# One layer of causal attention and routed experts: 64-row operands in 128-partition transfers, and steps moved

## The chip, the cores and the metric

The kernel runs on one core of one Trainium2 chip. The metric is the device time of one execution in microseconds (us), lower is better. A core has five engines that run their own instruction streams and meet at semaphores: TensorE (PE, matrix products), VectorE (DVE), ScalarE (ACT), GpSimd (POOL) and SyncE (SP, which here only issues transfers).

## The reference

For 8 batches of 512 tokens and 128 features the output is x plus causal attention plus a mixture of experts, both on the layer norm of x:

```python
xn = _layernorm(x, axis=-1)
x = x + attention(xn) + ffn(xn)
# attention: 16 heads of 8 features
q, k, v = split(xn @ w_in.T + b_in)
attn = softmax(q * scale @ k.T + causal_bias)
out = (attn @ v) @ w_out.T + b_out          # NaN replaced by 0
# ffn: 8 experts of width 176, the best 2 of a token count, and shared experts of width 352
scores = softmax(x @ gate_w.T); topk_w = topk_w / topk_w.sum() * 2.5
y = sum_e combine[:, e] * (silu(x @ w_gate[e]) * (x @ w_up[e])) @ w_down[e]
y = y + (silu(x @ sw_gate) * (x @ sw_up)) @ sw_down
```

## The kernel before

The kernel works batch by batch. A batch i has two stages. `attend(i)` (L686 on PE, L807 on ACT, L949 on POOL, L1287 on DVE) computes 20 units of transposed scores (`scores_t`, L570), exponentiates each (L821), masks them on POOL (L946) and multiplies them with v (`weigh_v`, L605); beside it the tokens of batch i+1 get their projections, their splits into bf16 parts and their routing weights. `experts_and_maxima(b)` (L648 on PE, L1246 on DVE, `experts` L780 on ACT and L912 on POOL) runs the hidden features of the experts of batch b in 14 tiles, k = 0 to 13, and the row maxima of batch b's scores, 20 pairs of heads (`pair`, of `scores` L518 and `maxima` L1158), between them. PE's order inside a step k of that loop is: `gate_up(k)`, the pairs of the step, at k = 14 `project_k`, `scores_t(b, 0, 0)`, `project_v_and_logits`, at k = 15 `scores_t(b, 0, 1)`, then `down(k - 2)`, and at k = 12 (`MAXIMA_AT`) `transpose_x` and `transpose_maxima`.

A tile k goes gate_up (PE) -> silu (ACT, L763) -> times the routing weight, on POOL, if the tile is routed (L902) -> `hidden`, times up (DVE, L1141) -> high part (ACT L770, the last two DVE L1149) -> low part (POOL L908, the last three DVE L1156) -> down (PE, L495 to L497). Tiles 0 to 10 are routed, 11 to 13 shared; tile 13 has 96 rows. The order of all batches is 11, 12, 13, 0, ..., 10.

Scores are products of q and k that are split into three bf16 parts each: 6 products of parts (`TERMS`) times 8 features make 48 rows for a head, and the head's parity picks partitions 0 or 64. The parts go out to DRAM (`k_parts_out`, `q_parts_out`, L341 and L346) and come back as rows of `q_op` and `k_op` (`operands_in`, L362), in two halves of four transfers, each of 48 partitions. The maxima are reduced by DVE, split into three bf16 parts (`split_maxima`, L1175, four dependent instructions of 64 columns), transposed by PE (L555), copied by ACT into `max_rows` (L791), and brought by two transfers into three further rows of q_op for each parity (`maxima_in`, L382); rows 48 to 50 of k_op hold ones. `scores_t` waits for that (L574).

SP works through one queue in program order: parts out, first half of the operands, routing weights out to DRAM and back as `cb` (L360, 18 transfers a batch), second half, output, maxima. In the first batch ACT issues the routing weights itself (`weights_out`, L772), after high_hidden(2), and waits for them to be in DRAM before its next instruction. DVE normalises the tokens of the next batch (`normalise`, L1033) at the start of `experts_and_maxima`, ahead of the first maximum; only for the second batch it does it at k = 9.

Until the seventh maximum pair the pairs use one slot of PSUM, so that each `scores` waits until DVE has read the pair before it (L538).

## Time and profile before

| | us |
|---|---|
| median of 3 runs (612.55 to 613.24) | 613.1 |
| the profiled execution | 613.62 |
| its span on the core | 611.8 |
| PE busy | 534.0 (87%) |
| DVE busy | 489.3 (80%) |
| ACT busy | 342.0 (56%) |
| POOL busy | 343.9 (56%) |
| granted TensorE clock, mean | 0.973 |

Seven batches follow each other at 69.9 us (the first maximum pair of two neighbours starts at 390.24 and 460.17), after a start of some 37 us and the first batch's experts, and the last batch's attend stage ends the run. A stretch in the rows below gives its length and the busy time of each engine with the number of instructions, then the granted clock, the busy share of the 16 DMA engines and GB/s. A row of the timeline has the start, the duration, the engine, the line, the operation with its tiles and shapes, and in brackets how long the engine was idle before it and what ended that. Matmuls are pipelined: two of 0.39 us follow each other 0.23 us apart.

### The profile page before, as it was taken

The page shows a single profiled execution, that of the slowest core. Times are in us where ns is not written, and L with a number is a line of the kernel's source. Part 1 is how long each engine was busy: PE and PEld are TensorE (multiplying, and loading weights), DVE is VectorE, ACT ScalarE, POOL GpSimd, SP SyncE. Part 2 cuts the span into 40 slices and gives each one's busy share as a digit, 9 for nine tenths or more (in the row PEclk, how much of TensorE's full clock was granted, in tenths as well). Part 3 has the DMA queues.
Part 4 walks back from the last instruction along what each step waited for, and adds up shares of the span by engine and source line. Part 5 has one row for each costly group of instructions (what it writes and reads, how often), then busy time and mean ns, then how long its engine had stood idle before and what let it go on. Part 6 is the DMA issues. An engine that isn't in the chain of part 4 may idle for free.

```text
span 611.8 us, 13262 instructions
## 1 busy us (share of the span) xinstructions
PE 534.0 (87%) x4568; PEld 299.5 (49%) x4568; DVE 489.3 (80%) x802; ACT 342.0 (56%) x462; POOL 343.9 (56%) x363
## 2 busy tenths in 40 slices
PE   2737989997899989999898989899898998999894
PEld 2415742665326662466425663366525663366422
DVE  5956978899778978799778978799778988589513
ACT  5412378453883459534793459634694358734591
POOL 3145735385365854478355864568355773568442
PEclk9768999999999999999999999999999999999897
DMA  9655014700238003730147003630048003460001
GB/s 274 190 169 116 2 56 126 218 7 0 94 104 217 7 4 130 187 95 0 52 129 233 3 3 109 184 119 0 3 155 228 29 0 108 129 183 2 4 1 34
DMA packets 43198, 56.65 MB, mean 93 GB/s; under 512 B 4545, under 2 KB 28577, under 8 KB 43169
## 3 DMA queue, kind: packets, MB, share of 16 engines
q1 hardware_dynamic: 40460, 53.02, 29.6%
q10 hardware_dynamic: 2708, 3.24, 1.6%
q8 instruction: 18, 0.29, 0.2%
q14 instruction: 12, 0.09, 0.1%
HBM read 41.05 MB, written 14.81 MB: 91 GB/s over the span
## 4 chain that ended last, share of the span: by engine, by line
PE 56%; DVE 14%; ACT 10%; issue 8%; DMA 5%; POOL 4%; SPq 1%; ACTq 1%; DVEq 0%; POOLq 0%
PE banks L617 10%; PE banks L514 7%; PE banks L479 6%; ACT probs L821 6%; DVE neg_max L1166 6%; PE banks L590 6%; PE banks L481 5%; PE banks L480 5%; PE banks L495 5%; DMA q_op<-max_rows 3%; PE banks L496 3%; PE banks L497 3%; POOL hid_lo L908 2%; DVE probs L1141 2%; POOL probs L902 2%
## 5 line engine op out<-in xcount | busy, mean ns | idle before, releaser
L1166 DVE TENSOR_REDUCE neg_max<-banks 128x2 f32<-128x1024 f32 (+3 forms) x224 | 194.9, 915 | 15.4 <-PE banks L505 14.1
L821 ACT ACTIVATE probs<-banks 128x1024 f32<-128x1024 f32 x160 | 155.5, 1031 | 23.0 <-PE banks L590 20.8
L902 POOL TENSOR_TENSOR probs<-probs,cb 128x512 f32<-128x512 f32 x88 | 112.9, 1283 | 79.2 <-ACT probs L763 71.0
L946 POOL TENSOR_SCALAR_AFFINE_SELECT probs<-probs 128x512 f32<-128x512 f32 x128 | 91.6, 739 | 112.1 <-ACT probs L821 112.1
L763 ACT ACTIVATE probs<-banks 128x512 f32<-128x512 f32 (+1 forms) x112 | 66.9, 598 | 153.0 <-PE banks L481 145.8
L908 POOL TENSOR_TENSOR hid_lo<-probs,hid_hi 128x512 fp32r<-128x512 f32 (+1 forms) x88 | 113.5, 1289 | 62.0 <-ACT hid_hi L770 62.0
L1141 DVE TENSOR_TENSOR probs<-probs,banks 128x512 f32<-128x512 f32 (+1 forms) x112 | 75.9, 679 | 28.6 <-POOL probs L902 26.2
L479 PE MATMUL banks<-x_hi,w_hi 128*128 128x512 f32 (+1 forms) x224 | 94.5, 422 | 4.1 <-DVE probs L1141 2.4
L617 PE MATMUL banks<-probs,v_op 128*32 128x512 f32 (+3 forms) x1024 | 95.5, 445 | 0.6 <-POOL probs L946 0.4
L770 ACT ACTIVATE hid_hi<-probs 128x512 fp32r<-128x512 f32 (+1 forms) x96 | 60.5, 630 | 58.6 <-DVE probs L1141 58.1
L480 PE MATMUL banks<-x_lo,w_hi 128*128 128x512 f32 (+1 forms) x224 | 89.0, 397 | 0.0
L481 PE MATMUL banks<-x_hi,w_lo 128*128 128x512 f32 (+1 forms) x224 | 88.8, 396 | 0.0
L590 PE MATMUL banks<-q_op,k_op 51*128 51x384 bf16 (+3 forms) x512 | 63.0, 303 | 21.9 <-DMA q_op<-max_rows 11.4
L514 PE MATMUL banks<-k_op,q_op 48*64 48x512 bf16 (+3 forms) x1024 | 61.8, 310 | 20.6 <-DVE neg_max L1166 16.4
L590 PEld LDWEIGHTS banks<-q_op,k_op 51*128 51x128 bf16 x512 | 17.4, 94 | 95.4 <-ACT probs L821 56.9
L495 PE MATMUL banks<-hid_hi,wd_hi 128*128 128x512 f32 (+1 forms) x112 | 55.9, 499 | 9.2 <-POOL hid_lo L908 9.0
L514 PEld LDWEIGHTS banks<-k_op,q_op 48*64 48x64 bf16 x1024 | 24.3, 106 | 59.7 <-issue 57.3
L479 PEld LDWEIGHTS banks<-x_hi,w_hi 128*128 128x128 f32 (+1 forms) x224 | 42.3, 189 | 22.5 <-issue 6.8
L481 PEld LDWEIGHTS banks<-x_hi,w_lo 128*128 128x128 f32 (+1 forms) x224 | 42.4, 189 | 10.5
L480 PEld LDWEIGHTS banks<-x_lo,w_hi 128*128 128x128 f32 (+1 forms) x224 | 42.5, 190 | 8.4 <-issue 0.2
L497 PE MATMUL banks<-hid_lo,wd_hi 128*128 128x512 f32 (+1 forms) x112 | 45.2, 403 | 0.0
L496 PE MATMUL banks<-hid_hi,wd_lo 128*128 128x512 f32 (+1 forms) x112 | 45.2, 403 | 0.0
(122 smaller groups left out, 599.9 us busy)
## 6 DMA issues: line engine op xcount, KB each, us to landing
cb<-c_dram SPq DMA_DIRECT2D x31, 256.0 KB, 4.3
q_op<-q_dram SPq DMA_DIRECT2D x32, 192.0 KB
k_op<-k_dram SPq DMA_DIRECT2D x32, 192.0 KB
cb<-c_dram SPq DMA_DIRECT2D x16, 224.0 KB, 4.9
q_dram<-q_parts SPq DMA_DIRECT2D x8, 384.0 KB, 2.5
k_dram<-k_parts SPq DMA_DIRECT2D x8, 384.0 KB, 2.6
cb<-c_dram SPq DMA_DIRECT2D x16, 192.0 KB, 4.1
cb<-c_dram SPq DMA_DIRECT2D x15, 160.0 KB, 4.4
```

The source lines that it names most:

```text
L479: pe.matmul(bank, w_hi[:, w, cols], x_hi[:, :], start=True, stop=False)
L480: pe.matmul(bank, w_hi[:, w, cols], x_lo[:, :], start=False, stop=False)
L481: pe.matmul(bank, w_lo[:, w, cols], x_hi[:, :], start=False, stop=True).then_inc(ready, 1)
L514: pe.matmul(bank[rows, a, at:at + n], q_op[own, h // 2, qt * P + HALF * c:qt * P + HALF * (c + 1)], k_op[own, h // 2, 0:n], start=first, s ...
L590: mm = pe.matmul(bank[:, at:at + S - kb * P], k_op[r:r + rows, h // 2, kb * P:(kb + 1) * P], q_op[r:r + rows, h // 2, kb * P:S], start=Tru ...
L617: mm = pe.matmul(bank[32 * j:32 * j + 32, kb * P:S], v_op[:, kb, g % 2, 4 * (g // 2) + j, :], probs_of(g, j, kb), start=(c == 0 and g % 2 ...
L821: nc.scalar.activation(probs[:, g % 2, 2 * u:2 * u + 2, :], ring[:, at:at + 2, :], ACT.Exp).then_inc(exp_done, 1)
L902: nc.gpsimd.tensor_tensor(sg[k % 3][:, :], sg[k % 3][:, :], cb[:, tiles_of(b)[k], :], ALU.mult).then_inc(weighted, 1)
L908: nc.gpsimd.tensor_tensor(hid_lo[0:n, k % 3, :], hid[k % 3][0:n, :], hid_hi[0:n, k % 3, :].bitcast(F32), ALU.subtract).then_inc(hid_lo_don ...
L946: return nc.gpsimd.affine_select(out=view, in_=view, compare_op=ALU.is_ge, fill=0.0, base=0, pattern=[[0, 4], [1, P]], channel_multiplier=-1)
L1141: nc.vector.tensor_tensor(hid[k % 3][0:n, :], sg[k % 3][0:n, :], ring[0:n, up_bank(k), :], ALU.mult).then_inc(hid_done, 1)
L1166: return nc.vector.tensor_reduce(out, in_, AX.X, ALU.max, negate=True)
```

## The change

- Heads get 64 rows, 8 slots for each of the 8 features, laid out feature by feature (row = 8 d + slot): slots 0 to 5 the products, slot 6 the maxima, slot 7 nothing (q 0, k 1). q_dram and k_dram have 8 slots; slots 6 and 7 are written once at the start by two transfers from memory set by POOL. `operands_in` issues two transfers of 128 partitions instead of four of 48. `maxima_in` issues one transfer, into 16 partitions, from a `max_rows` of 128 rows of which 5 of 8 are zero.
- `split_maxima` has seven dependent `tensor_reduce` (copies over an axis of one, subtraction as the sum of two, one of them negated) instead of two copies and two subtractions.
- Batches after the first take their tiles as 11, 12, 0, ..., 10, 13.
- At k = 12 PE transposes the maxima ahead of down(10) and transpose_x; ACT copies max_rows ahead of high_hidden and take_xT. `project_v_and_logits` stands ahead of `scores_t(b, 0, 0)`; take_k ahead of the first exponential, exp_router after the second.
- For batches 2 to 6 `normalise` stands in attend, after the routing weights, instead of at the start of the experts.
- First batch: the split of one half of the routed weights (`low_routed(1)`), the high part of the down weights on ACT, the routing weights and their way out each stand elsewhere: router_weights at k = 1, transpose_comb at k = 2 behind down(0), weights_out after high_hidden(1), `low_down` on POOL waits for routed_lo.

```diff
-TILES_LATER = TILES_FIRST
+TILES_LATER = list(range(ROUTED, NT - 1)) + list(range(ROUTED)) + [NT - 1]
...
-                for s in range(2):
-                    rows = slice(HALF * s, HALF * s + SROWS)
-                    sp.dma_start(q_op[rows, own, :], q_dram[:, s, :, own, :]).then_inc(ops_loaded[n], 16)
-                    sp.dma_start(k_op[rows, own, :], k_dram[:, s, :, own, :]).then_inc(ops_loaded[n], 16)
+                for op, dram in ((q_op, q_dram), (k_op, k_dram)):
+                    sp.dma_start(op[:, own, :].rearrange("p i n -> p (i n)"),
+                                 dram[:, :, :, own, :].rearrange("t s d i n -> (s d) t (i n)")
+                                 ).then_inc(ops_loaded[n], 16)
...
-                for s in range(2):
-                    row, own = HALF * s + SROWS, MROWS * PAIRS * s
-                    sp.dma_start(q_op[row:row + MROWS, :, :], max_rows[own:own + MROWS * PAIRS, :]
-                                 ).then_inc(m_loaded, 16)
+                sp.dma_start(q_op[TERMS:P:SLOTS, :, :], max_rows[:, :]).then_inc(m_loaded, 16)
...
+            sp.wait_ge(slots_set, 3)
+            sp.dma_start(q_dram[TERMS:SLOTS].rearrange("t s d i n -> (s d i) t n"), q_op[:, 0:SLOTS - TERMS, :]
+                         ).then_inc(slots_written, 16)
+            sp.dma_start(k_dram[TERMS:SLOTS].rearrange("t s d i n -> (s d i) t n"), k_op[:, 0:SLOTS - TERMS, :]
+                         ).then_inc(slots_written, 16)
...
                     if k == NT:
                         if front:
                             project_k(b + 1)
+                            project_v_and_logits(b + 1, vl)
                         scores_t(b, 0, 0)
-                        if front:
-                            project_v_and_logits(b + 1, vl)
                     if k == NT + 1:
                         scores_t(b, 0, 1)
+                    if k == MAXIMA_AT:
+                        transpose_maxima(b)
                     if k >= 2:
                         down(b, k - 2, i)
+                    if k == 2 and i is None:
+                        transpose_comb(0)
...
-                    if k == MAXIMA_AT:
-                        if front:
-                            transpose_x(b + 1)
-                        transpose_maxima(b)
+                    if k == MAXIMA_AT and front:
+                        transpose_x(b + 1)
...
                     if k == NT - 2:
+                        act.wait_ge(mT_ready, b + 1)
+                        nc.scalar.activation(max_rows[:, :], bank_m[:, 0:S // 2].bitcast(BF16), ACT.Copy
+                                             ).then_inc(mrows_done, 1)
                         high_hidden(b, k - 1)
                         if front:
                             take_xT(b + 1)
...
-            nc.gpsimd.memset(k_op[:, :, :], 1.0).then_inc(ones_set, 1)
+            nc.gpsimd.memset(q_op[:, 0:SLOTS - TERMS, :], 0.0).then_inc(slots_set, 1)
+            nc.gpsimd.memset(k_op[:, 0:SLOTS - TERMS, :], 1.0).then_inc(slots_set, 1)
+            nc.gpsimd.memset(max_parts[:, :, :, :, :], 0.0).then_inc(slots_set, 1)
...
+                def over_one(out, in_, negate):
+                    return nc.vector.tensor_reduce(out, in_.unsqueeze(4), AX.X, ALU.max, negate=negate)
+
+                def of_two(out, in_):
+                    return nc.vector.tensor_reduce(out, in_, AX.X, ALU.add)
...
+                then(over_one(max_parts[:, :, :, 0, :], neg_max[:, :, :, :, 0], False))
+                then(over_one(neg_max[:, :, :, :, 1], max_parts[:, :, :, 0, :], True))
+                then(of_two(max_rest[:, :, :, :, 0], neg_max[:, :, :, :, :]))
+                then(over_one(max_parts[:, :, :, 1, :], max_rest[:, :, :, :, 0], False))
+                then(over_one(max_rest[:, :, :, :, 1], max_parts[:, :, :, 1, :], True))
+                then(of_two(max_last[:, :, :, :], max_rest[:, :, :, :, :]))
+                over_one(max_parts[:, :, :, 2, :], max_last[:, :, :, :], False).then_inc(msplit_step, 1)
...
-                    if front and i is not None and k == (9 if second else 0):
+                    if second and k == 9:
                         normalise(b + 1)
...
                 if front:
                     router_weights(i + 1)
+                    if middle:
+                        normalise(i + 2)
                     take_combT(i + 1)
```

## Rows read from the trace of the kernel before

**Rows 1.** Stretches of a middle batch: length, busy PE, PEld, DVE, ACT, POOL; clock, DMA share.

```profile
389.90:402.70 12.80, 11.08 (x110) 6.81 (x103) 11.05 (x17) 4.53 (x8) 6.45 (x10) 1.00 0.93 245
402.70:427.30 24.60, 24.60 (x236) 17.04 (x235) 23.79 (x32) 9.77 (x16) 19.45 (x16) 1.00 0.06 24
...
441.10:459.80 18.70, 17.39 (x179) 5.00 (x177) 14.26 (x29) 18.16 (x21) 10.29 (x15) 1.00 0.38 130
```

**Rows 2.** Timeline of PE, from the end of gate_up(12) to the first transposed scores.

```profile
430.13 0.39 PE L481 MATMUL banks<-x_hi,w_lo 128*128 128x512 f32 x1
430.88 0.50 PE L495 MATMUL banks<-hid_hi,wd_hi 128*128 128x512 f32 x1 [0.37 <-POOL hid_lo L908]
...
437.03 0.39 PE L590 MATMUL banks<-q_op,k_op 51*128 51x512 bf16 x2 [1.27 <-DMA q_op<-max_rows]
437.35 1.19 PE L445 MATMUL banks<-wvg_sb,xnT 128*128 128x136 f32 x8
```

**Rows 3.** Timeline of ACT in the same stretch: maxima, first and third exponential.

```profile
432.82 0.58 ACT L791 ACTIVATE max_rows<-banks 48x512 bf16<-48x512 bf16 x1
...
437.46 1.02 ACT L821 ACTIVATE probs<-banks 128x1024 f32<-128x1024 f32 x1 [1.80 <-PE banks L590]
...
441.08 1.03 ACT L821 ACTIVATE probs<-banks 128x1024 f32<-128x1024 f32 x1
```

**Rows 4.** Timeline of SP's queue: the two transfers of the maxima.

```profile
433.42 1.58 SPq L386 DMA_DIRECT2D q_op<-max_rows  x2
```

**Rows 5.** The chain that ended last, in order of time: start, duration, what.

```profile
31.10 5.43 DMA c_dram<-combT
...
37.43 5.25 DMA cb<-c_dram
...
434.26 2.65 DMA q_op<-max_rows
```

**Rows 6.** Timeline of DVE: the split of the maxima, and the last tile's hidden features.

```profile
427.78 0.40 DVE L1181 CAST max_parts<-neg_max 128x64 bf16<-128x64 f32 x1
...
429.67 1.24 DVE L1188 TENSOR_TENSOR max_parts<-max_rest,max_parts 128x64 bf16<-128x64 f32 x1
...
435.69 0.69 DVE L1141 TENSOR_TENSOR probs<-probs,banks 128x512 f32<-128x512 f32 x1 [2.12 <-POOL probs L902]
```

**Rows 7.** Timeline of POOL in the same stretch.

```profile
429.55 1.29 POOL L908 TENSOR_TENSOR hid_lo<-probs,hid_hi 128x512 fp32r<-128x512 f32 x1
```

**Rows 8.** A reduction from SBUF to SBUF on DVE: durations in ns, min/median/max.

```profile
L1116 DVE TENSOR_REDUCE rt<-rt_pair x8: 419/420/420, 28.6 to 519.4; 128x32 f32<-128x256 f32 x8
```

**Rows 9.** Timeline of DVE: normalise and low_routed in the first batch; a middle batch.

```profile
9.22 1.12 DVE L1038 TENSOR_SCALAR xn<-x_sb,ln 128x128 f32<-128x128 f32 x4
...
15.47 3.15 DVE L1338 TENSOR_TENSOR w_lo<-probs,w_hi 128x1408 fp32r<-128x1408 f32 x2
...
389.90 3.17 DVE L1038 TENSOR_SCALAR xn<-x_sb,ln 128x128 f32 x4
392.57 1.21 DVE L1166 TENSOR_REDUCE neg_max<-banks 128x2 f32<-128x1024 f32 x1
...
453.00 0.28 DVE L1129 COPY combT<-banks 32x128 f32<-32x128 f32 x1 [1.47 <-PE banks L452]
```

**Rows 10.** Timeline of PE: the second maximum pair of the batch.

```profile
393.93 0.41 PE L514 MATMUL banks<-k_op,q_op 48*64 48x512 bf16 x4 [1.29 <-DVE neg_max L1166]
```

**Rows 11.** One us of operand loads, one of cb loads, as in rows 1.

```profile
384.00:385.00 1.00, 1.00 (x10) 0.10 (x2) 1.00 (x2) 1.00 (x2) 1.00 (x2) 1.00 0.37 147
...
398.00:399.00 1.00, 1.00 (x11) 0.68 (x13) 1.00 (x3) 0.48 (x1) 0.00 (x0) 1.00 1.07 270
```

**Rows 12.** Timeline of PE at the ends of the first, second and last batch's experts.

```profile
78.04 0.38 PE L560 MATMUL banks<-ident_bf,max_parts 128*48 128x128 bf16 x4 [1.10 <-DVE max_parts L1188]
...
156.83 0.39 PE L590 MATMUL banks<-q_op,k_op 51*128 51x512 bf16 x2 [1.88 <-DMA q_op<-max_rows]
...
575.27 0.39 PE L590 MATMUL banks<-q_op,k_op 51*128 51x512 bf16 x2 [1.93 <-DMA q_op<-max_rows]
```

More of the change, by code:

```diff
@@ L147, in block_kernel @@
         v_op = sb("v_op", [P, QT, 2, H // 2, 32])
-        neg_max = sb("neg_max", [P, QT, 2, PAIRS])
-        max_rest = sb("max_rest", [P, QT, 2, PAIRS])
-        max_parts = sb("max_parts", [P, QT, 2, MROWS, PAIRS], BF16)
-        max_rows = sb("max_rows", [3 * H, S], BF16)
+        neg_max = sb("neg_max", [P, QT, 2, PAIRS, 2])
+        max_rest = sb("max_rest", [P, QT, 2, PAIRS, 2])
+        max_last = sb("max_last", [P, QT, 2, PAIRS])
+        max_parts = sb("max_parts", [P, QT, 2, DH, PAIRS], BF16)
+        max_rows = sb("max_rows", [P, S], BF16)
         probs = sb("probs", [P, 2, NAT, S])
@@ L590, in scores_t @@
                         mm = pe.matmul(bank[:, at:at + S - kb * P],
-                                       k_op[r:r + rows, h // 2, kb * P:(kb + 1) * P],
-                                       q_op[r:r + rows, h // 2, kb * P:S], start=True, stop=True)
+                                       k_op[r:r + HALF, h // 2, kb * P:(kb + 1) * P],
+                                       q_op[r:r + HALF, h // 2, kb * P:S], start=True, stop=True)
                 mm.then_inc(st_ready, 1)
@@ L789, in experts @@
                             take_xT(b + 1)
-                        act.wait_ge(mT_ready, b + 1)
-                        nc.scalar.activation(max_rows[:, :], bank_m[0:3 * H, 0:S // 2].bitcast(BF16), ACT.Copy
-                                             ).then_inc(mrows_done, 1)
+                    if i is None and k == 1:
+                        high_routed_down()
                     if 1 <= k < NT - LATE_HIGH:
                         high_hidden(b, k - 1)
-                    if i is None and k == 3:
+                    if i is None and k == 2:
                         weights_out()
@@ L1173, in maxima, with then @@
                 else:
-                    last = neg(neg_max[:, 1, :, 2 * g:2 * g + 2], bank[:, :, :].rearrange("p a (k n) -> p a k n", k=2))
+                    last = neg(neg_max[:, 1, :, 2 * g:2 * g + 2, 0], bank[:, :, :].rearrange("p a (k n) -> p a k n", k=2))
                 last.then_inc(nat_max, 1)
             def split_maxima(b):
+                n = [0]
+                def then(ins):
+                    n[0] += 1
+                    ins.then_inc(msplit_step, 1)
+                    dve.wait_ge(msplit_step, MSPLIT_STEPS * b + n[0])
@@ L1252, in experts_and_maxima @@
                         split_maxima(b)
+                    if k == 1 and i is None:
+                        router_weights(0)
                     if k == 2 and i is None:
-                        router_weights(0)
+                        take_combT(0)
+                        low_routed(1)
+                        constants()
                     if k == 3 and i is None:
-                        take_combT(0)
-                        constants()
                         normalise(1)
@@ L1287, in attend @@
                 second = isinstance(i, int) and i == 0
+                middle = not isinstance(i, int)
                 if front:
@@ L1323, in low_shared, with low_routed @@
                                             wd_hi[rows, tiles, :].bitcast(F32), ALU.subtract).then_inc(shared_lo, 1)
+            def low_routed(w):
+                dve.wait_ge(w_hi_done, w + 2)
+                nc.vector.tensor_tensor(w_lo[:, w, 0:SPLIT], w_raw[:, w, 0:SPLIT], w_hi[:, w, 0:SPLIT].bitcast(F32),
+                                        ALU.subtract).then_inc(routed_lo, 1)
             statistics(0)
@@ L1335, in _ @@
             take_v(0, vl_first)
-            for w in range(2):
-                dve.wait_ge(w_hi_done, w + 2)
-                nc.vector.tensor_tensor(w_lo[:, w, 0:SPLIT], w_raw[:, w, 0:SPLIT], w_hi[:, w, 0:SPLIT].bitcast(F32),
-                                        ALU.subtract).then_inc(routed_lo, 1)
+            low_routed(0)
             split_q(0)
```

55 lines of the change are left out of this document (23 added, 32 removed).

## The prediction, made before the changed kernel was built or run

> **What bounds it now.** The busy shares of the page put PE first with 87% of the span and DVE next with 80%, but no engine is full for the whole batch, so I read one middle batch in stretches [rows 1]. In attend ACT is busy for 18.16 of 18.70 us: the 20 exponentials bound that stage, and it ends a fixed time after the third of them has started. In the body of the experts PE is busy for all of 24.60 us and DVE for 23.79: nothing that I move can shorten it. That leaves the seams, where PE waits. At the start of the experts PE is busy for 11.08 of 12.80 us; its second pair waits 1.29 us for a maximum [rows 10], which DVE starts late since normalise, 3.17 us, stands before it [rows 9]. At the end PE waits 0.37 us for a low part and 1.27 us for the maxima's transfer [rows 2], and ACT idles 1.80 us before its first exponential [rows 3]. I therefore price the change by what it does at these two seams, batch by batch, and at the start. The granted clock is 1.00 in the stretches of the middle batch, the higher of its two levels, 2.4 GHz [rows 1]; I leave it there.
>
> **End of the experts, a middle batch.** From the end of gate_up(12) (430.13 plus the 0.23 at which matmuls follow each other, 430.36) to the first transposed scores at 437.03 PE takes 6.67 us [rows 2]. Of these, 0.37 and 1.27 are waits. The transposes of the maxima now stand where the 0.37 was; the other steps are the same, and project_v, 1.19 us by its row and some 1.0 until the next can start, comes ahead of the scores. PE is thus ready at 430.36 + 6.67 - 0.37 - 1.27 + 1.0 = 436.4, if the maxima are there: 0.6 earlier. Are they? The split starts at 427.78 and ends at 430.91 [rows 6]. Its last instruction ends within 0.1 us of POOL's, 429.55 + 1.29 [rows 7], and has only 64 columns: it sat out POOL's instruction. The nearest row for the new steps is a reduction of 256 columns from SBUF, 419 to 420 ns in all 8 cases [rows 8], never stretched. One of 1024 columns takes 1.21 [rows 9], so 768 columns cost 0.79, and 256 of the 0.42 are 0.26, 0.16 fixed: 64 columns 0.22 us, 128 columns 0.29; five and two of them make 1.7 us, with six gaps of under 0.1 (the old split's 3.13 us hold three of them) some 1.9 to 2.2. The split ends near 429.8, ahead of the 430.36 at which PE comes to it. ACT copies max_rows at 430.9 instead of 432.82 [rows 3], 1.9 earlier. From that copy's end to the landing it takes 3.5 us (433.40 to 434.26 + 2.65) [rows 4, 5]; one transfer is issued instead of two, which saves between nothing and 0.8. The rows land at 434.2 to 435.0, over 1 us before PE asks. The copy of 128 rows instead of 48 has the same 512 columns and stays at 0.58.
>
> Then the exponentials. From the first scores to the start of the third exponential it takes 437.03 to 441.08, 4.05 us [rows 3]. The copy of k leaves that stretch (it now falls in the idle 1.80), and the second scores wait only for one down step: scores 0.4, exponential 1.0, exponential 1.0, copy of y 0.6, exp_router 0.2 make 3.2 to 3.4. I take 3.3, a gain of 0.75. This needs hidden(13) early: DVE waits 2.12 us for POOL to weigh the last tile and has it at 435.69 [rows 6]. A shared last tile isn't weighed, and all four instructions behind it end before 437. Its bound if that cover is gone is the 0.75. So the end gives 0.6 + 0.75 = 1.35, between 0.6 and 2.0.
>
> **Start of the experts, batches 2 to 6.** Without normalise, which starts at 389.90, DVE takes the first maximum as soon as PE has it, some 1.7 before 392.57, and the second pair goes 1.29 earlier [rows 9, 10]; the pairs are chained one by one, so I carry 1.25 on, between 0.6 and 2.0. In attend normalise costs 1.12 (undisturbed) to 3.17 us; DVE idles 1.47 there, waiting for combT [rows 9], and more later, and ACT bounds. I take nothing; up to 0.4 if its o_sb comes late. The 18 cb transfers behind combT run at a share of 1.07 [rows 11] and are wanted by tile 0, now at k = 2; POOL, busy 6.45 of 12.80 in that stretch [rows 1], has room for the weighing: nothing.
>
> **The other batches.** Batch 1 waits 1.88 for its maxima [rows 12]: 0.6 more than the middle ones, of which PE gets back all but project_v: 0.9, and 0.75 at the exponentials: 1.7. The last batch has no projections; its wait of 1.93 [rows 12] goes almost whole, and about 1.1 at the exponentials, 3.0. In the first batch the split comes at k = 12 and PE already waits 1.10 for it [rows 12]. Here down(10) and transpose_x stand behind that wait now, 1.3 us of work that covered it: its scores come 1.2 later, less 0.75 behind them: a loss of 0.5 (0 to 1.2).
>
> **Start of the run.** The chain goes through combT's way to DRAM, 5.43 us from 31.10, and cb's, 5.25 us from 37.43 [rows 5]. combT comes 2.2 us earlier: half of the 3.15 of low_routed [rows 9] and one `hidden`, 0.69 [rows 6], no longer stand before it. I count 2.1. It is queued with the operand loads; these run at a DMA share of 0.37 and 147 GB/s, others at 1.07 and 270 [rows 11]. If 128 partitions go as those do, 1 MB takes 3.9 us instead of 768 KB in 5.3, in half as many issues, and combT's write waits less. I take 3.5 us, between 2.1 (order alone) and 5. The two transfers of slots cost SP about 1 us ahead of q_parts_out; it had idled there for that long. POOL's memory sets shrink.
>
> On the shares of the DMA engines the Trainium skill, "DMA: Bandwidth & Descriptors", section "Why a DMA increments its semaphore by 16 and not by 1", says that a transfer runs on the largest number of engines up to 16 that divides the slowest dimension of both sides: six for the old operands (6 terms), and 6 of 16 is the 0.37 of rows 11; 16 for the new. Without that rule the new form could as well keep 147 GB/s, 1 MB taking 7 us, and the start would gain 2.1 or less.
>
> **Sum.** 5 x (1.35 + 1.25) = 13.0; batches 1 and last 1.7 + 3.0; batch 0 minus 0.5; start 3.5: 20.7 us. The profiled span of 611.8 would become 591.1 (its execution 613.62 - 20.7 = 592.9); off the median of 613.1 it gives 592.4 us.
>
> **Rivals.**
> *Slower: the seven steps stall PE.* Were reductions held up by POOL like the copies they replace, each would take up to 1.24 [rows 6], seven 8.7 us, and the split would end at 436.5. Behind it on PE stand down(10), transpose_x, gate_up(13) and all the rest, 6.0 us less the 0.3 that fill: first scores at 442, 5 us late and some 4.5 us in the end, in eight batches 36, against 9.8 from the start and normalise: 640 us. It decides from a split longer than 2.6 us (427.78 to 430.36) and turns the sign near 5. Against it: the flat 419 to 420 ns while POOL works [rows 8]. The Trainium skill, "SBUF — State Buffer", states that on trn2 a tensor_reduce never contends for the port pair shared with GpSimd, while a copy, or a tensor_tensor with both inputs in SBUF, does; by the opposite rule this rival would be the forecast. 6%.
> *The end gains only PE's wait.* The exponentials keep their spacing because the next down or y comes late: 0.6 us at each end, 0 at some: 7 x 0.75 less, 598 us. For it: ACT's queue at k = 12 is now copy, high part, xT, silu, and a late silu moves everything behind. 17%.
> *Normalise only moves.* DVE is busy 14.26 of 18.70 in attend [rows 1] and order matters there: late combT or o_sb delays PE's transposes and the scores behind them; 5 x 1.25 less: 598.6; with the rival before it 604. 10%.
> *The wide transfers aren't faster.* The start gains at most 2.1 and the operands take 7 us: nothing else waits for them in a middle batch; 594 to 596. 7%.
> *More than forecast.* Removing DVE work in a stretch where it is busy 11.05 of 12.80 [rows 1] gives 2.0 a batch, and the start 5: 587. 10%.
>
> **Numbers.** The forecast itself (589 to 596) has 50%. The range holds all but the slow rival and the worst pair: 586 to 602. What a measurement of this kernel can tell from no change is 0.2%, 1.2 us; faster 0.92, same 0.02, slower 0.06.
>
> **What would show it.** Right: the seven split steps below 0.3 us each; no PE wait for q_op<-max_rows in batches 1 to 7, the projections of v ahead of the scores; first exponentials 3.3 us apart; the second pair without a wait for neg_max; a period of 67.3 us; a DMA share near 1 for operands; first cb some 3.5 us before 42.7. Wrong: split steps over 1 us, a PE wait at L560 beyond the first batch, a period of 69 or more, or new waits of ACT at k = 12 and 13.

## The result and the profile after

The changed kernel takes 590.66 us (median of 4 runs, 590.21 to 591.25), the kernel before beside it 613.05 (612.55 to 613.24): ratio 0.9637, 95% interval 0.9620 to 0.9653. The prediction was 592.4 in 586 to 602. The profiled execution took 591.25 us, its span is 589.3, 22.5 less than before.

To see where the time went I took one mark in every batch, the start of its third exponential, in both traces; from there the attention stage runs at ScalarE's pace. The shift of that mark from batch to batch is finer than any median, because what happens at the start of the run drops out of it. It is still one execution of each kernel, and a stretch of low granted clock that only one of them has stays in it.

| third exponential of batch | before | after | shift | gained in this batch | forecast |
|---|---|---|---|---|---|
| 0 (start of the run included) | 86.70 | 84.17 | -2.53 | 2.53 | 3.0 |
| 1 | 160.89 | 156.44 | -4.45 | 1.92 | 1.7 |
| 2 | 231.22 | 223.43 | -7.79 | 3.34 | 2.6 |
| 3, 4, 5, 6 | 441.08 (5) | 424.37 (5) | -16.71 (5) | 3.00, 2.96, 2.96, 2.94 | 2.6 each |
| 7 | 579.96 | 557.01 | -22.95 | 3.30 | 3.0 |

Two rows hold such a stretch. In batch 1 the changed kernel's granted clock is 0.50, the lower of its two levels (1.2 GHz), from 138.7 to 142.1 us, and the kernel before has none there: the 1.92 would be some 0.5 larger without it (experiment 1). In the last batch it is the other way round: the clock of the kernel before falls to 0.50 at 575.7, behind PE's wait of 1.93 us [rows 12], and 1.20 of the 3.30 us come behind the first scores, where its products take 0.63 us each and not 0.39.

Stretches of a middle batch of the changed kernel, cut at the same work as in [rows 1]: the first part of its experts, their body, attend (columns as in [rows 1]), and then 2 us of operand loads in the first batch.

```profile
376.15:387.50 11.35, 10.93 (x109) 6.86 (x102) 8.50 (x13) 4.46 (x7) 7.70 (x11) 1.00 1.01 240
387.50:412.10 24.60, 24.60 (x237) 17.06 (x236) 23.83 (x32) 9.84 (x16) 19.41 (x16) 1.00 0.16 40
424.40:443.10 18.70, 17.27 (x179) 4.99 (x177) 14.92 (x31) 18.17 (x21) 10.19 (x15) 1.00 0.60 169
30.00:32.00 2.00, 2.00 (x6) 1.63 (x5) 2.00 (x3) 0.63 (x2) 2.00 (x2) 0.50 1.03 223
```

Against [rows 1] body and attend are as long and as full as they were. The first stretch lost 1.45 us and DVE 2.55 us of work in it. In attend DVE has 0.66 more, and ACT's 18.17 of 18.70 still set the pace. The DMA share of operand loads is 1.03 where it was 0.37 [rows 11].

The seam at the end of the same batch, DVE (start, duration, line, operation):

```profile
412.61 0.21 DVE L1196 TENSOR_REDUCE max_parts<-neg_max 128x64 bf16<-128x64 f32 x1
412.85 0.22 DVE L1196 TENSOR_REDUCE neg_max<-max_parts 128x64 f32<-128x64 bf16 x1
413.11 0.29 DVE L1199 TENSOR_REDUCE max_rest<-neg_max 128x64 f32<-128x128 f32 x1
...
414.26 0.22 DVE L1196 TENSOR_REDUCE max_parts<-max_last 128x64 bf16<-128x64 f32 x1
...
417.10 0.69 DVE L1150 TENSOR_TENSOR probs<-probs,banks 128x512 f32<-128x512 f32 x1 [1.80 <-POOL probs L911]
...
418.60 0.68 DVE L1150 TENSOR_TENSOR probs<-probs,banks 96x512 f32<-96x512 f32 x1 [0.21 <-ACT probs L765]
```

The split takes 1.87 us (412.61 to 414.48) in seven steps of 0.21 to 0.29; it took 3.13 in four [rows 6]. The last tile's hidden features at 418.60 no longer wait for POOL, where they had waited 2.12 us; the wait, now 1.80, stands at the tile before it, at 417.10. PE in the same place:

```profile
414.94 0.39 PE L485 MATMUL banks<-x_hi,w_lo 128*128 128x512 f32 x1
415.17 0.40 PE L564 MATMUL banks<-ident_bf,max_parts 128*128 128x128 bf16 x4
415.72 0.50 PE L499 MATMUL banks<-hid_hi,wd_hi 128*128 128x512 f32 x1
...
420.11 1.09 PE L449 MATMUL banks<-wvg_sb,xnT 128*128 128x136 f32 x8
421.13 0.39 PE L593 MATMUL banks<-q_op,k_op 64*128 64x512 bf16 x2
```

No line carries a wait in brackets. Of [rows 2] the 0.37 (the transposes now stand in it) and the 1.27 are gone, project_v stands ahead of the scores, and these come 15.90 us earlier than at 437.03 while gate_up(12) ends 15.19 earlier: 0.71 gained. ACT:

```profile
415.61 0.60 ACT L794 ACTIVATE max_rows<-banks 128x512 bf16<-128x512 bf16 x1 [0.32 <-PE banks L564]
...
421.56 1.02 ACT L831 ACTIVATE probs<-banks 128x1024 f32<-128x1024 f32 x1 [0.56 <-PE banks L593]
422.85 1.02 ACT L831 ACTIVATE probs<-banks 128x1024 f32<-128x1024 f32 x1 [0.27 <-PE banks L593]
...
424.37 1.03 ACT L831 ACTIVATE probs<-banks 128x1024 f32<-128x1024 f32 x1
```

From the first scores to the third exponential it takes 3.24 us, where [rows 2, 3] have 4.05. The start of the same batch, PE:

```profile
378.82 0.41 PE L518 MATMUL banks<-k_op,q_op 64*64 64x512 bf16 x4
```

The second pair, which waited 1.29 us in [rows 10], has no wait.

The chain that ended last, at the start of the run (start, duration, what):

```profile
27.66 0.19 ACT hid_hi L772
27.85 2.00 DMA c_dram<-combT
...
30.75 9.48 DMA cb<-c_dram
...
40.30 1.26 POOL probs L911
```

combT's way to DRAM begins 3.2 us earlier than in [rows 5] and takes 2.00 us, not 5.43. But cb's takes 9.48, not 5.25, so POOL gets its first share only 2.45 us earlier than at 42.75 (3.2 + 3.4 - 4.2). The longer reads are what the prediction had not seen.

### The profile page after: what moved, and what is told of

Same layout as the page of the kernel before. It is cut to its first block, busy times and chain, and to the rows that moved or that the text cites. A ratio compares the mean times of both kernels' runs of the same rounds, so it can differ in the third digit from the quotient of the medians.

```text
span 589.3 us, 13270 instructions
## 1 busy us (share of the span) xinstructions
PE 530.7 (90%) x4568; PEld 300.3 (51%) x4568; DVE 471.7 (80%) x826; ACT 342.2 (58%) x462; POOL 343.6 (58%) x365
## 3 DMA queue, kind: packets, MB, share of 16 engines
q10 hardware_dynamic: 2708, 3.24, 1.7%
## 4 chain that ended last, share of the span: by engine, by line
PE 62%; DVE 14%; ACT 9%; issue 8%; POOL 4%; DMA 3%; ACTq 0%; DVEq 0%; POOLq 0%
PE banks L620 11%; PE banks L483 7%; PE banks L518 7%; ACT probs L831 6%; PE banks L499 6%; PE banks L485 6%; PE banks L484 6%; PE banks L593 6%; DVE neg_max L1175 5%; PE banks L500 3%; PE banks L501 3%; DVE probs L1150 2%; POOL hid_lo L917 2%; DMA cb<-c_dram 2%; POOL probs L911 2%
## 5 line engine op out<-in xcount | busy, mean ns | idle before, releaser
L772 ACT ACTIVATE hid_hi<-probs 128x512 fp32r<-128x512 f32 (+1 forms) x96 | 60.4, 630 | 50.9 <-DVE probs L1150 50.6
L593 PE MATMUL banks<-q_op,k_op 64*128 64x384 bf16 (+3 forms) x512 | 62.8, 302 | 11.3 <-ACT probs L831 11.3
L518 PE MATMUL banks<-k_op,q_op 64*64 64x512 bf16 (+3 forms) x1024 | 60.4, 306 | 12.0 <-DVE neg_max L1175 10.4
L593 PEld LDWEIGHTS banks<-q_op,k_op 64*128 64x128 bf16 x512 | 17.4, 93 | 79.5 <-ACT probs L831 57.4
L518 PEld LDWEIGHTS banks<-k_op,q_op 64*64 64x64 bf16 x1024 | 23.6, 105 | 49.8 <-issue 47.3
```

The costliest lines, as they stand in the source:

```text
L518: pe.matmul(bank[rows, a, at:at + n], q_op[own, h // 2, qt * P + HALF * c:qt * P + HALF * (c + 1)], k_op[own, h // 2, 0:n], start=first, s ...
L593: mm = pe.matmul(bank[:, at:at + S - kb * P], k_op[r:r + HALF, h // 2, kb * P:(kb + 1) * P], q_op[r:r + HALF, h // 2, kb * P:S], start=Tru ...
```

## The experiments

In all of them "per batch" is the shift of the third exponential against the trace of the changed kernel. Each edit is made in the changed kernel. Beside them the kernel before took 613.67 us (normalise back, tile order, old split, the start's old order), 613.13 (project_v, k = 12, both, four transfers), 612.53 (copy of the keys, weight reads ahead, second half ahead of the reads) and 613.87 (write issued by SP).

### 1. What each moved step is worth in a batch

**Normalise back ahead of the first maximum.**

```diff
-                    if second and k == 9:
+                    if front and i is not None and k == (9 if second else 0):
...
-                    if middle:
-                        normalise(i + 2)
```

> The changed kernel with normalise for batches 2 to 6 back at the start of the experts. Theory of the prediction: PE's second pair waits 1.3 us again in five batches, 590.7 + 5 x 1.25 to 1.4 = 597 to 598. Rival, the move only shifted work that something else hid: under 592. Rival, DVE is what bounds the experts, so all of its 3.2 us come back: 603 to 607.

Measured 596.95 us (596.72 to 600.37), ratio 0.9745 (0.9715 to 0.9774). Shift of batch 1 -1.23, then 0.12, 1.49, 2.85, 4.20, 5.56 and 5.58: 1.35 us in each of batches 2 to 6, nothing in 1 and 7. Its DVE and PE at the start of the batch:

```profile
378.99 3.16 DVE L1047 TENSOR_SCALAR xn<-x_sb,ln 128x128 f32 x4
381.66 1.21 DVE L1175 TENSOR_REDUCE neg_max<-banks 128x2 f32<-128x1024 f32 x1
```

```profile
383.01 0.41 PE L518 MATMUL banks<-k_op,q_op 64*64 64x512 bf16 x4 [1.30 <-DVE neg_max L1175]
```

The old wait is back with its old size, and the whole of it reaches the end of the batch. In attend normalise costs nothing that lasts: there it takes 1.14 us, and PE and ACT are not held up.

**The shared tile last in the routed order, undone.**

```diff
-TILES_LATER = list(range(ROUTED, NT - 1)) + list(range(ROUTED)) + [NT - 1]
+TILES_LATER = TILES_FIRST
```

> The changed kernel with the old order of tiles in all batches (the last one routed). Theory: DVE gets the last tile 1.3 to 2 us later, the last two down steps and with them the second and third exponential come up to 0.75 us late in seven batches: 593 to 596. Rival, the last tile's weighing was hidden behind other waits of DVE: within 1 us of 590.7.

Measured 596.58 us (593.83 to 597.31), ratio 0.9717 (0.9690 to 0.9745). Per batch 0.28 to 0.45 in batches 1 to 6, and 1.97 in the last, 4.3 in all behind batch 0, in one execution; the medians lie 5.9 apart. In its trace the last tile's hidden features wait again, and so does the second exponential:

```profile
422.22 0.69 DVE L1150 TENSOR_TENSOR probs<-probs,banks 128x512 f32<-128x512 f32 x1 [1.61 <-POOL probs L911]
```

```profile
425.43 1.02 ACT L831 ACTIVATE probs<-banks 128x1024 f32<-128x1024 f32 x1 [0.63 <-PE banks L593]
```

The 1.61 us become 0.4 at the exponentials; where the rest goes I have not followed. In the last batch, which has no projections, PE waits 1.64 us for a low part at 558.59 and its second scores come 1.27 us late. The other 0.7 come behind them: this trace's granted clock falls to 0.50 at 559.9, which the changed kernel's does not.

**The split of the maxima in four steps again.**

```diff
-        MSPLIT_STEPS = 7
+        MSPLIT_STEPS = 4
...
+                then(nc.vector.tensor_copy(max_parts[:, :, :, 0, :], neg_max[:, :, :, :, 0]))
+                then(nc.vector.tensor_tensor(max_rest[:, :, :, :, 0], neg_max[:, :, :, :, 0],
+                                             max_parts[:, :, :, 0, :], ALU.subtract))
...
```

> The changed kernel with the split of the maxima as two copies and two subtractions again (in the new layout). Theory: it takes 3.1 us beside POOL instead of 1.9, ends 0.6 us after PE has come to it, and hidden(11) starts 1.2 later: 0.5 to 1.0 us in six or seven batches, 594 to 598. Rival, the split is off the path in either form: within 1 us of 590.7.

Measured 590.79 us (589.35 to 592.26), ratio 0.9631 (0.9607 to 0.9655). Per batch 0.12 to 0.16 in batches 2 to 6, 0.37 in the last. Its DVE:

```profile
411.50 0.39 DVE L1203 CAST max_parts<-neg_max 128x64 bf16<-128x64 f32 x1
411.92 0.23 DVE L1204 TENSOR_TENSOR max_rest<-neg_max,max_parts 128x64 f32<-128x64 f32 x1
412.18 1.19 DVE L1206 CAST max_parts<-max_rest 128x64 bf16<-128x64 f32 x1
413.41 1.24 DVE L1207 TENSOR_TENSOR max_parts<-max_rest,max_parts 128x64 bf16<-128x64 f32 x1
```

Two of the four steps are stretched from under 0.4 to 1.2 us while POOL works; none of the seven reductions above is, beside the same POOL instructions. So the reason for writing a copy as a reduction is real, but it is worth 0.14 us a batch: PE waits 0.57 us for the split and would have waited for POOL's low part right behind it anyway. The rival (off the path) was right. The Trainium skill, "SBUF — State Buffer", section "Who interferes with whom", says that on trn2 a tensor_reduce never contends for the port pair shared with GpSimd, while a copy can. The rows agree: 0.21 to 0.29 us for each reduction, 1.19 for the second copy; the first copy, 0.39, was not held up.

**project_v behind the first scores; the old order at k = 12; both.**

```diff
-                            project_v_and_logits(b + 1, vl)
                         scores_t(b, 0, 0)
+                        if front:
+                            project_v_and_logits(b + 1, vl)
```

```diff
-                    if k == MAXIMA_AT:
-                        transpose_maxima(b)
...
-                    if k == MAXIMA_AT and front:
-                        transpose_x(b + 1)
+                    if k == MAXIMA_AT:
+                        if front:
+                            transpose_x(b + 1)
+                        transpose_maxima(b)
```

The second edit also puts ScalarE's copy of max_rows back behind its high part and xT.

> The changed kernel with project_v_and_logits behind the first transposed scores again. Theory of the prediction: its work fills a wait for the maxima, so the wait comes back, 0.6 us or more in each of six batches: 594 to 596. Rival: with the earlier maxima alone there is no wait left to fill (they land 1 us ahead of 420.1), the first exponential even starts 1 us earlier and the second is where it was: third exponential within 0.3 us a batch, 589.5 to 592.

> The changed kernel with the old order at k = 12: PE transposes x and then the maxima behind down(10), ACT copies max_rows behind high_hidden and take_xT. Theory: the hole of 0.3 us at down(10) is open again and the maxima leave 2 us later, behind which project_v still covers: 0.3 to 0.6 us a batch, 592.5 to 595. Rival: the order at k = 12 is the gain at the end and it goes whole, 1.2 us a batch or more: 598 or above.

> Both of the two edits before together. If each covers for the other, the wait for the maxima is back only here: 1.2 to 1.6 us in six or seven batches, 599 to 602. If they add up: the sum of what the two showed alone.

Measured: project_v behind, 591.66 us (589.30 to 593.22), 0.00 per batch. Old order at k = 12, 590.78 (588.78 to 591.78), 0.03 to 0.07 per batch in batches 2 to 6 (-0.49 in batch 1, 0.38 in the last). Both, 593.24 (590.93 to 594.11), ratio 0.9665 (0.9631 to 0.9699), 0.54 to 0.58 per batch in batches 2 to 6. Each alone is worth nothing, the two together 0.57: either brings the maxima in ahead of PE, and only without both does PE wait. (The -0.49 in batch 1 is the clock: this trace does not have the changed kernel's 0.50 from 138.7 to 142.1.) In the trace of both:

```profile
422.50 0.39 PE L593 MATMUL banks<-q_op,k_op 64*128 64x512 bf16 x2 [0.46 <-DMA q_op<-max_rows]
```

With project_v behind, the first exponential comes 0.67 us earlier, the second then waits 0.95 for its scores, and the third starts when it did. I had expected 1.2 to 1.6 for the pair.

**The copy of the keys back behind the first exponential.**

```diff
-                if front:
-                    take_k(i + 1)
...
-                            if (g, u) == (0, 1):
+                            if (g, u) == (0, 0):
+                                take_k(i + 1)
                                 exp_router(i + 1)
```

> The changed kernel with the copy of the keys and the router's exponential back behind the first exponential on ScalarE, as in the kernel before. Theory 1 (the exponentials lie 3.24 us apart rather than 4.05 because this copy no longer stands between them): the third exponential comes 0.5 to 0.8 us later in each of the seven batches with a successor, +3.5 to +5.5 us in all: 594 to 596 us. Theory 2 (the copy then runs while ScalarE waits for the scores of the second unit anyway): 0 to 0.1 us per batch, 590.2 to 591.5 us.

Measured 590.36 us (589.97 to 593.90), ratio 0.9650 (0.9625 to 0.9675). 0.15 to 0.27 per batch in batches 1 to 6, 0.20 in the mean, between the two theories and nearer to the second. exp_router moved with the copy, so the 0.2 are those of both. Of the 0.81 us by which the exponentials drew together, 0.2 are these two and 0.67 project_v's place, which alone only holds the first exponential back and leaves the third where it was. The prediction had named both, and put the weight on the copy.

### 2. The start of the run

**The start's steps in their old order.**

```diff
-                    if i is None and k == 2:
+                    if i is None and k == 3:
                         weights_out()
...
-                pool.wait_ge(routed_lo, 2)
+                pool.wait_ge(router_step, ROUTER_STEPS)
...
+            low_routed(1)
             split_q(0)
```

With it transpose_comb, high_routed_down, router_weights, take_combT and constants go back too.

> The changed kernel with the steps of the first batch in their old order (routing weights at k = 2, combT at k = 3, both halves of low_routed ahead of the split, high part of the down weights ahead of take_k), transfers as in the changed kernel. Theory: combT leaves 3 us later and the whole run moves by what the start had gained, 2 to 3 us: 592.7 to 593.7. Rival, the wide transfers gave the start its gain and the order nothing: within 0.8 us of 590.7.

Measured 593.61 us (593.08 to 594.56), ratio 0.9679 (0.9659 to 0.9699). The shift is 3.39 at batch 0 and 3.26 to 3.35 in all others: the order is worth some 3 us. That does not leave nothing for the wide transfers, although batch 0's third exponential (87.56) is no earlier than before the change (86.70). POOL's first share starts at 41.88 here, at 42.75 before the change and at 40.30 in the changed kernel, so of the 2.45 us up to there the order has 1.58 and the wide transfers 0.87: combT's write, issued at 30.90 and not 31.10, takes 4.43 us and not 5.43, the reads 5.58 and not 5.25. The other 1.8 of the 3.39 come behind the share. This trace's granted clock is 0.50 up to 50.6 us, the changed kernel's up to 46.5, and here it is so once more from 77.9 to 81.3 (columns as in [rows 1]):

```profile
78.00:81.30 3.30, 3.30 (x11) 2.60 (x11) 0.69 (x1) 1.80 (x4) 0.00 (x0) 0.50 0.15 40
```

Whether the old order brings these stretches on is not shown.

**Weight reads ahead of the second half of the operands.** SP issues the second reads and the second 1 MB of operands once the first reads have landed.

```diff
-            sp.wait_ge(comb_written, 16)
+            sp.wait_ge(cb_loaded[0], 16 * len(SEGMENTS[0]))
             weights_around(1)
             operands_in(0, None, 1)
```

> One wait of SP is longer than in the changed kernel, in the first batch only: it issues the second group of weight reads and the second half of the operands once the first five weight reads have landed, not once the routing weights were written. Theory 1: in the changed kernel the first weight reads took 9.5 us (30.75 to 40.24) where they took 5.25 before, because the second half of the operands (1 MB, issued 32.7 to 33.9) shares the queues' engines with them; held back, the reads land in 5 to 7 us, hidden(3) comes up to 3 us earlier than 41.60, and the third exponential of batch 0 and everything behind it moves by -1.3 to -3.0 us: 587.7 to 589.4 us against 590.7. Theory 2: the first half, issued at 28.1 to 29.5 ahead of the reads, is what they queue behind; then nothing moves by more than 0.5 us, or the start grows by up to 1 us because the second half now lands later: 590 to 592 us.

Measured 587.97 us (586.69 to 588.74), ratio 0.9586 (0.9565 to 0.9607): its interval lies below that of the changed kernel. The shift is -2.27 at batch 0 and -2.35 to -2.39 in all others. Its chain:

```profile
27.97 5.77 DMA c_dram<-combT
34.62 3.48 DMA cb<-c_dram
```

With nothing behind them, the reads take 3.48 us and not 9.48. But the trace says a second thing: the write takes 5.77 here and took 2.00 in the changed kernel's. Nothing of this edit comes ahead of it. Across the traces the write goes with what was issued first: where ScalarE issued it 0.26 us or more ahead of SP's first operands (27.85 against 28.11; 28.26 against 28.62) it took 2.0 us, and where it came with them or behind (27.93 against 27.74, 27.95 against 27.78, 27.95 against 27.95) 4.3 to 4.8, once 7.2. Where it was late, the second half of the operands, which waits for it, was late too, and in six of seven such kernels the reads were quicker: POOL had its first share at 38.5 to 39.2 (in the seventh at 41.69), earlier than the 40.30 of the changed kernel's own trace. So the start has a race between two queues, and a single trace of it is only good to some 2 us: the kernels whose edits do not touch the start had batch 0 at -2.03 to +0.70 us against the trace of the changed kernel. Part of that is the clock: the trace with the old tile order has its first share 1.29 us earlier and its third exponential 0.70 later, with a granted clock of 0.50 up to 51.3 and not 46.5. Of the 2.3 us of this experiment the traces therefore show only what lies below 38.5 (the share at 38.17); that the kernel is faster rests on the medians, of different sets of runs.

**The write issued by SP just ahead of the operands**, on top of the last edit, so that the race is decided.

```diff
+            sp.wait_ge(combT_done, 1)
+            sp.dma_start(c_dram.rearrange("e (q n) -> q e n", q=QT), combT[:, :]).then_inc(comb_written, 16)
             operands_in(0, None, 0)
...
-                act.wait_ge(combT_done, 1)
-                act.dma_start(c_dram.rearrange("e (q n) -> q e n", q=QT), combT[:, :]).then_inc(comb_written, 16)
```

> The kernel whose second operand half waits for the first weight reads (588.0 us), and in it the write of the routing weights issued by SP just ahead of the first half of the operands, instead of by ScalarE at about the same time. Theory 1: in the traces so far the write took 2.0 us where it was issued at least 0.26 us ahead of the operands (27.85 against 28.11) and 4.4 to 5.8 us where it came after them; ahead of them for certain, it lands at 30 and the three weight reads, issued at 30 and not at 33.8, land with the operands at 36.3 to 37 and not at 38.1: the first share of batch 0 starts 1.2 to 1.9 us earlier than 38.17, the third exponential of batch 0 by as much, 586.1 to 586.8 us. Theory 2: reads issued while 1 MB of operands is in flight take turns with it and end no earlier than those issued behind it (9.5 us, as in the changed kernel): share at 38 to 39.5, 588 to 589.3 us.

Measured 589.95 us (587.65 to 590.65), ratio 0.9612 (0.9589 to 0.9634); its profiled execution, 587.65, is the shortest of the five. SP and POOL:

```profile
28.23 0.66 SPq L409 DMA_DIRECT2D c_dram<-combT  x1
```

```profile
37.69 1.26 POOL L911 TENSOR_TENSOR probs<-probs,cb 128x512 f32<-128x512 f32 x1 [2.31 <-DMA cb<-c_dram]
```

The write lands 2 us later, at 30.2, as expected, but the first share comes at 37.69, only 0.5 before the 38.17 of the last experiment: reads issued at 30.2 end hardly earlier than reads issued at 33.8; the first 1 MB of operands is issued ahead of both. The third exponential of batch 0 is at -2.49, later ones at -3.1, as this trace too lacks the low clock in batch 1. The intervals of the two kernels overlap, so which is faster stays open.

### 3. Is it the width of the transfers?

**Four operand transfers of 64 partitions instead of two of 128.** The same bytes in the same operand rows; features go outermost, 8 of them. There are also twice as many transfers to issue, some 0.6 us of SP each, which this test does not tell apart from the width.

```diff
...
+                for s in range(2):
+                    for op, dram in ((q_op, q_dram), (k_op, k_dram)):
+                        sp.dma_start(op[HALF * s:HALF * (s + 1), own, :].rearrange("p i n -> p (i n)"),
+                                     dram[:, s, :, own, :].rearrange("t d i n -> d t (i n)")
...
```

> The changed kernel with the operands in four transfers of 64 partitions for each half, the 8 features outermost. By the rule on the number of DMA engines these run on 8 of 16: a DMA share of 0.5 while they run alone, 1 MB in 5.3 us at 200 GB/s. Theory: in the middle batches nothing waits for them, 0; at the start cb, which took 9.5 us behind them, comes earlier or later by up to 1 us: 590 to 592.5. Rival, the width carries gain in each batch: 593 or above.

Measured 603.18 us (602.08 to 606.88), ratio 0.9850 (0.9805 to 0.9896). The shift is 3.39 at batch 0, then 4.22, 5.86, 6.89, 7.66, 9.25, 12.06, 12.89. Over half of the change's gain is gone, and most of that in batches where I had seen no operand on the path. The share of the DMA engines during the loads is 0.52 (one of 31.00 to 32.00 us), half of the changed kernel's 1.05 in the same stretch. That is 8 of 16 engines and 16 of 16: by the rule of the Trainium skill, "DMA: Bandwidth & Descriptors", section "Why a DMA increments its semaphore by 16 and not by 1", that the prediction weighed, the trace agrees. SP's queue in a middle batch of this kernel:

```profile
375.51 0.57 SPq L376 DMA_DIRECT2D k_op<-k_dram  x1
377.21 0.65 SPq L357 DMA_DIRECT2D c_dram<-combT  x1
384.30 8.69 SPq L362 DMA_DIRECT2D cb<-c_dram  x18
393.19 0.63 SPq L376 DMA_DIRECT2D q_op<-q_dram  x1
```

and of the changed kernel:

```profile
369.55 0.68 SPq L357 DMA_DIRECT2D c_dram<-combT  x1
372.76 8.68 SPq L362 DMA_DIRECT2D cb<-c_dram  x18
381.63 0.55 SPq L375 DMA_DIRECT2D q_op<-q_dram  x1
```

From the write to the first read it takes 7.1 us here, 3.2 in the changed kernel and 4.4 before the change (383.38 to 387.78); in all seven such batches 6.7 to 7.7, 3.0 to 4.0 and 4.4 to 6.0. The write, 16 KB, stands behind 1 MB of operands that were issued just ahead of it. SP waits for it, then needs 8.7 us to issue the 18 reads, and only then comes the second half of the operands. PE gets to it first:

```profile
404.87 0.41 PE L519 MATMUL banks<-k_op,q_op 64*64 64x512 bf16 x4 [1.20 <-DMA k_op<-k_dram]
...
474.66 0.41 PE L519 MATMUL banks<-k_op,q_op 64*64 64x512 bf16 x4 [2.17 <-DMA k_op<-k_dram]
```

Six such waits after the start make 5.6 us of the 9.5 by which the later batches shifted. Most of the other 3.9 lies at the same pair, the first of the second half, in batches 1 and 2, which shift by 1.6 us each there:

```profile
128.29 0.41 PE L519 MATMUL banks<-k_op,q_op 64*64 64x512 bf16 x4 [1.35 <-DVE neg_max L1176]
```

The trace puts this wait, and one of 1.40 us in batch 2, down to DVE. But in the changed kernel the same pair has no wait, and here it starts 9.5 and 10.0 us after the last load was issued, as where the trace names k_op (9.0 to 10.8). So it too is most likely the operands. The changed kernel has one wait for k_op, 1.55 us at 36.26.

**The same, with the second half issued ahead of the reads.**

```diff
-                weights_out(i + 1)
+                sp.wait_ge(combT_done, i + 2)
+                sp.dma_start(c_dram.rearrange("e (q n) -> q e n", q=QT), combT[:, :]).then_inc(comb_written, 16)
+                operands_in(i + 1, i, 1)
+                sp.wait_ge(comb_written, 16 * (i + 1) + 16)
                 for m in range(len(CB_GROUPS)):
                     weights_around(m)
-                operands_in(i + 1, i, 1)
```

> The kernel with four operand transfers of 64 partitions (603.2 us), and in it the second half of the operands issued right behind the write of the routing weights, ahead of its landing and of the 18 weight reads, instead of behind them. Theory 1: TensorE's waits for k_op in batches 1 to 6 (5.6 us in six waits, the longest 2.17 at 474.66) come from the second half being issued only after the reads; they go, and of the 9.5 us that this kernel loses between the third exponential of batch 0 and that of batch 7 five to six return: 597 to 598.5 us. Theory 2: the engines of the queue are the limit, not the order of the issues; then the weight reads land later by as much, GpSimd or VectorE waits for cb, and the time stays at 601 to 604 us.

Measured 634.07 us (633.23 to 636.26), ratio 1.0342 (1.0316 to 1.0368): slower than the kernel before, and 31 us slower than the last one. The waits for k_op go, as the first theory had it (0.5 us in two waits is left of 5.6 behind the first), but POOL waits for cb in all eight, 59.0 us:

```profile
418.47 1.26 POOL L914 TENSOR_TENSOR probs<-probs,cb 128x512 f32<-128x512 f32 x1 [7.34 <-DMA cb<-c_dram]
```

In this batch the reads are issued 7.8 us after the write (397.99 to 405.78), barely later than before the edit. They land late with 1 MB just ahead of them. The rate of the DMA engines is the limit, as the second theory had it, and I had put too low a price on it: two waits of about 1 us were traded for one of 7. Part of the 31 us is the clock that follows the waits. Between 203 and 572 us the granted clock falls to 0.50 six times, for 27 us together, where the kernel with the second half behind the reads stays at 1.00:

```profile
203.10:206.50 3.40, 3.40 (x19) 2.40 (x18) 2.14 (x3) 0.00 (x0) 2.17 (x2) 0.50 0.71 218
```

With products 0.42 us apart and not 0.23, that is at most some 12 us (an estimate).

## Why the prediction came out right, step by step

The time and the period (66.97 us, from one batch's first silu at 377.88 to the next at 444.85; forecast 67.3) are those forecast. By its terms:

- **Start of the experts, 1.25 a batch.** Shown: 1.35 by undoing it, and 1.44 between the two traces up to gate_up(12) (-13.75 to -15.19), batches 2 to 6 only. The rival that normalise only moves is refuted: DVE has 0.66 us more work in attend and nothing waits for it.
- **End of the experts, 0.6 + 0.75.** In the traces 0.71 + 0.81. The size is right, but the causes are in part others, and to that extent the match is luck. The 0.6 is shared: the order at k = 12 and project_v's place cover for each other (0.0, 0.05, together 0.57). Of the 0.75 I had put most on the copy of k, which with exp_router is 0.2; the rest is project_v no longer standing between the first two scores, and hidden(13) being early, 0.4 by the tile order. Undone one at a time, tile order, both places, copy and split make 0.4 + 0.57 + 0.2 + 0.14 = 1.3 of 1.5; the remaining 0.2 I have not assigned. That the end would gain only PE's wait was wrong.
- **Seven steps that stall PE** (the slower rival): refuted. 1.87 us against 1.9 to 2.2 forecast, from reductions of another size. What I had not priced is how little the split matters: the old one costs 0.14 a batch and 0.37 in the last.
- **Batch 1, 1.7; the last, 3.0.** 1.92 and 3.30, the first with some 0.5 lost and the second with up to 1.2 gained by a stretch of low clock in one of the two traces, which the prediction had left out. Of the last, 1.97 is the tile order, 0.7 of it with the clock at 0.50.
- **Batch 0, a loss of 0.5.** PE's wait for the split grew from 1.10 [rows 12] to 2.41 us, 1.3 against 1.2 forecast. The third exponential nevertheless moved as much as POOL's first share did (2.53 and 2.45). But the loss is there, and something else covers it: in the kernel with the old order at k = 12 this wait is 1.27 us, and from the first share to the third exponential it takes 42.93 us and not 43.87.

```profile
74.32 0.38 PE L564 MATMUL banks<-ident_bf,max_parts 128*128 128x128 bf16 x4 [1.27 <-DVE max_parts L1196]
```

  The order costs batch 0 some 0.9 us. From the first to the third exponential it takes 3.14 us and not 3.55, which gives back 0.41 where 0.75 was forecast; the rest I have not assigned.
- **Start, 3.5, of which 2.1 the order.** The total is 2.5 in the trace, and 1 to 2 more in those traces where the race went the other way. Its division was wrong: combT left 3.2 us earlier and not 2.1, nearly all of it by the order. That "combT's write waits less" holds, 4.43 us for 5.43 with the old order and 2.00 in the changed kernel's own trace. The step that failed is the one behind it, which the sum put at nothing: that cb's reads keep their 5.25 us. With a second megabyte issued beside them they took 9.48. I had followed the write behind the operands and not the reads that come after it.
- **The wide transfers aren't faster** (594 to 596 us): refuted at 1.03 of the engines. But this rival's reasoning, that nothing else waits for operands in a middle batch, was wrong, and mine had leaned on it too. At 8 engines the kernel is 12.5 us slower than at 16. The sum did not suffer, as at 16 there is no such wait; but I had the transfers' whole worth at 1.4 us, and the step from 16 to 8 engines is worth nine times that. What the change would give with its orders and the old layout of 6 engines I did not run.
- **More than forecast.** Batches 2 to 6 gave 15.2 for 13.0, for the reasons above; the start and batch 0 gave back 0.5. The sum is close partly because its errors have both signs.

## What to carry to other kernels

A small transfer that others depend on is as slow as the bulk around it: here 16 KB took between 2.0 and 7.2 us at the start, and the first reads of the routing weights 3.5 or 9.5. Ask of each bulk load not only who waits for it but which small transfers share the DMA engines with it. Placing the write first was not enough: the reads behind it then took the longer, and moving it for certain ahead brought no shorter time. What helped was to hold back the bulk that nobody wanted yet until the reads had landed (587.97 us, not 590.66). When two moves both shorten one wait, undo both before calling either worthless; and judge a small edit by its shift per batch between traces, as the median can drift by more than its worth.

## What I had not expected of the hardware

- Transfers issued from two engines' queues hold each other up: the loads keep all 16 DMA engines busy (a share of 1.03 to 1.05) and leave none free. The write of 16 KB took 2.00 us where ScalarE issued it at 27.85 and SP's first operands followed at 28.11, and 4.4 us where SP's came at 27.67 and the write at 27.85.
- Idle PE in the first batch is paid for twice. After 4.18 us without work its matrix products from 42.84 on take 0.63 us each and not 0.39 until 46.4. The first row is 3 us of that idle stretch, the second the products behind it (columns as in [rows 1]): the granted clock is 0.61, then 0.50, the lower of its two levels, 1.2 GHz. Such stretches differ from trace to trace and move the time by 0.5 to 2 us each, as above.

```profile
39.00:42.00 3.00, 0.00 (x0) 0.00 (x0) 1.73 (x4) 0.00 (x0) 1.70 (x2) 0.61 1.05 215
43.00:45.00 2.00, 2.00 (x5) 1.61 (x6) 0.69 (x1) 0.00 (x0) 2.00 (x2) 0.50 1.07 213
```
